# A transformer block on one core: the feed-forward weight splits in slots 10 to 15, the second statistics merge behind the residual, squares between exponentials, two low parts moved

## Chip, core and metric

The kernel runs on one core of a Trainium2 chip. The metric is the device time of one execution in microseconds; the median of three executions stands for the kernel. One more execution was recorded by the profiler, and all rows below are from it.

## What is computed

The reference takes x (128 sequences of 64 tokens, 256 features) and a condition vector for each sequence. It applies a conditioned layer norm and then one transformer block whose two halves are each modulated by the condition:

```python
x = _L0_cond_ref(x, cond_256, ...)              # layer norm, affine, + tanh(cond @ lin_w.T + lin_b)
a_alpha = (t @ attn_alpha_w.T)[:, None, :]
x = x + a_alpha * _attention(_ada_rmsnorm(x, t, attn_gamma_w, attn_beta_w), W_q, W_k, W_v, W_o)   # 16 heads of 16
f_alpha = (t @ ffn_alpha_w.T)[:, None, :]
return x + f_alpha * _swiglu(_ada_rmsnorm(x, t, ffn_gamma_w, ffn_beta_w), gate_w, hidden_w, out_w, out_b)
# _swiglu: silu(x @ gate_w.T) * (x @ hidden_w.T) @ out_w.T + out_b, 1024 hidden features
```

## The kernel before

The 8192 tokens are worked on in 32 parts of 256 tokens, four sequences each. The program of every engine is one loop over slots `s`; a slot handles one sequence of attention (two at a time, in even slots) and one of the 128 feed-forward steps, `f = s - FFN_AT` with `FFN_AT = 12`. `grp, j = s // 4, s % 4` say which part is in which stage. The order on an engine is the order of the code, and semaphores tie the engines together. The attention of part m starts in slot 4m, its feed-forward part in slot 4m + 12. So slots -8 to 11 are a lead-in with attention alone, and from slot 12 on TensorE has both. In slots below 12 (`wide(s)`) the row minimum is subtracted on VectorE (`centre`, L797) and one exponential a sequence runs on ScalarE (L1127); later eight exponentials a sequence run straight from PSUM (L1134).

All large products are made in three passes: each operand is split into a rounded high part (made on ScalarE, a copy to fp32r) and a low part, the difference (made on VectorE or GpSimd). The attention input's low part `xn_lo` is `split_lo_a` (L1344, GpSimd), the feed-forward input's is `xf_lo` (L869, VectorE).

The feed-forward weights are split in the same way, in 12 chunks of 128 x 512: 0 to 3 gate, 4 to 7 hidden, 8 to 11 output. The table `SPLITS` says in which slot: ScalarE makes the high part of a chunk at the end of its body of slot s (L1184), and VectorE the low part at the end of its body of the slot after, s + 1 (L940):

```python
for c in SPLITS.get(s if s < 0 else s - 1, ()) if s != 0 else ():
    split_ffn_weights(c)
```

TensorE waits for the low parts by the semaphore `ffn_lo_made`, which counts chunks in the table's order. `gate(0)` wants the count at chunk 6, `gate(2)` at chunk 3, and the down product of step f, for the first four steps, its own chunk:

```python
def down(f):
    m, q = f // PSEQ, f % PSEQ
    pe.wait_ge(prod_lo_made, f + 1)
    if f < PSEQ:
        pe.wait_ge(ffn_lo_made, split_no(8 + f))
```

In slot s, TensorE runs `gate(f)`, `hidden(f)` and then `down(f - 1)`. VectorE runs `activate(f)` (L876, after ScalarE's tanh L1157) and `product(f)` (L884, after hidden(f)), then token work on the input (`shift_tokens` L750 and L754, `token_stats` L716), and then the weight splits. `product_lo(f)` (L912) opens the next slot.

`merge_stats` (L723 to L733) makes mean and variance from the statistics of 512 tokens; seven instructions on 128 x 4 elements. The stage of part m in attention runs: `turn_x` on TensorE, `make_residual` (L782, VectorE), squares (L1053), their sum (GpSimd L1320) turned on TensorE (L418), their mean (L842, L845), the inverse root (GpSimd L1306), scale, beta, high part, low part. `square_f`, `sum_squares_f`, `scale_f`, L1357 and `split_hi_f` are the same for the feed-forward half; its squares are turned by L422.

Of the kernel before, what the change touches and what calls it, by code (L numbers as in the profile page):

```python
# [61 lines left out]
LAST_SLOT = FFN_AT + FFN_STEPS + 2  # L62
LAST_STEP = FFN_STEPS - 1
LATE_TURNS = (BATCH - PSEQ - 1, BATCH - 1)
SPLITS = {-3: (0, 2), -2: (4,), 1: (5,), 3: (7,), 5: (6,), 6: (8,), 9: (1,), 11: (3,), 12: (9,), 13: (10,), 14: (11,)}
SPLIT_ORDER = [c for chunks in SPLITS.values() for c in chunks]
OUT_W_AT = -3
QUAD = 32
# [3 lines left out]
def conditioned_block(nc, x, cond_t, mod_w, feat_vecs, attn_w, gate_w, hidden_w, out_w, identity, head_mask, out_t):  # L72
    with ExitStack() as ctx:
# [120 lines left out]
        def is_part(m):  # L194
            return 0 <= m < NPART

        def is_seq(g):
            return 0 <= g < BATCH
# [4 lines left out]
        def wide(g):  # L203
            return g < FFN_AT
# [505 lines left out]
        def _(dve):  # L710
# [112 lines left out]
            def attended_lo(m):  # L823
                dve.wait_ge(att_hi_made, m + 1)
                dve.tensor_tensor(kt_by_seq(att_lo[:]), attended_t, kt_by_seq(att_hi[:].bitcast(F32)), ALU.subtract
                                  ).then_inc(att_lo_made, 1)
# [35 lines left out]
            def scale_f(m):  # L862
                dve.wait_ge(inv_spread, m + 5)
                dve.wait_ge(gamma_f, m + 1)
                scale_by_rms(normed_f, PART).then_inc(scaled_f, 1)
# [97 lines left out]
            for s in range(FIRST_SLOT, LAST_SLOT):  # L963
# [23 lines left out]
                if j == 0 and is_part(grp + 2) and not PSEQ <= s <= FFN_AT and not row_part(grp + 2):  # L987
                    make_residual(grp + 2)
                if s == FFN_AT:
                    merge_stats((grp + 3) // 2, (grp + 3) // 2 + 2)  # L990
                if j == 2 and s >= 0 and is_part(grp + 2):
                    scale_a(grp + 2)
                if j == 2 and is_part(grp - 2) and not wide(s):
                    scale_f(grp - 2)
                if j == 2 and is_part(grp - 2) and wide(s):
                    scale_f(grp - 2)
                if j == 2 and is_part(grp - 1) and wide(s):
                    attended_lo(grp - 1)
                for g in (s, s + 1):
                    if s % 2 == 0 and is_seq(g) and wide(g):  # L1000
                        invert_sums(g)
# [33 lines left out]
                    shift_tokens(tile_at(s))  # L1035
                if grp % 2 == 0 and 2 <= (grp + 4) // 2 < NBLK:
                    token_stats((grp + 4) // 2, j)
                    if j == 3 and grp != 2:
                        merge_stats((grp + 4) // 2, (grp + 4) // 2 + 2)
                for c in SPLITS.get(s if s < 0 else s - 1, ()) if s != 0 else ():  # L1040
                    split_ffn_weights(c)

# [5 lines left out]
        def _(act):  # L1048
# [158 lines left out]
            for s in range(FIRST_SLOT, LAST_SLOT):  # L1207
# [27 lines left out]
                    keys_out(grp + 1)  # L1235
                if s == FFN_AT:
                    square_a(grp + 2)
                    keys_out(grp + 1)
                    square_f(grp - 2)
                if s % 2 == 0 and is_seq(s):  # L1240
                    exponentials(s)
                    if s == 2:
                        queries_out(1)
                    if wide(s) and j == 2 and is_part(grp - 1):
                        attended_hi(grp - 1)
                    if wide(s + 1):
                        exponentials(s + 1)
                if j == 0 and s >= 0 and is_part(grp + 2) and not PSEQ <= s <= FFN_AT and not row_part(grp + 2):
                    square_a(grp + 2)
                if j == 0 and is_part(grp - 2) and wide(s):  # L1250
                    square_f(grp - 2)
                if j == 2 and is_part(grp - 1) and not wide(s):
                    attended_hi(grp - 1)
                if j == 2 and PSEQ <= s < FFN_AT:
# [37 lines left out]
        def _(pool):  # L1292
# [49 lines left out]
            def split_lo_a(m):  # L1342
                pool.wait_ge(hi_a, m + 1)
                pool.tensor_tensor(xn_lo[:], normed_a[:], xn_hi[:].bitcast(F32), ALU.subtract).then_inc(lo_a, 1)  # L1344
# [42 lines left out]
            for s in range(FIRST_SLOT, LAST_SLOT):  # L1387
# [9 lines left out]
                    apply_beta_a(grp + 2)  # L1397
                for g in (s, s + 1):
                    if s % 2 == 0 and is_seq(g) and wide(g):
                        normalise_probs(g)  # L1400
                        if g == s and j == 2:
                            split_lo_a(grp + 2)
                if s == FIRST_SLOT or s == FIRST_SLOT + PSEQ:
                    sum_squares_a(grp + 2)
# [81 lines left out]
```

## Time and profile before

| | |
|---|---|
| median of three executions | 958.8 us (957.88 to 959.99) |
| profiled execution, its own time | 958.45 us |
| its span in the trace | 956.4 us |
| busy: TensorE, VectorE, ScalarE, GpSimd | 920.8, 742.4, 636.4, 499.9 us |
| TensorE busy in the first 100 us | 70.3 us |

The span is what the trace covers, from the first instruction to the last; the profiled execution's time is 2.05 us longer than its span. Times of rows are microseconds from the start of the span, durations of groups nanoseconds.

### The profile page before, as it was taken

The page shows a single profiled execution, that of the slowest core. Times are in us where ns is not written, and L with a number is a line of the kernel's source. Part 1 is how long each engine was busy: PE and PEld are TensorE (multiplying, and loading weights), DVE is VectorE, ACT ScalarE, POOL GpSimd, SP SyncE. Part 2 cuts the span into 40 slices and gives each one's busy share as a digit, 9 for nine tenths or more (in the row PEclk, how much of TensorE's full clock was granted, in tenths as well). Part 3 has the DMA queues.
Part 4 walks back from the last instruction along what each step waited for, and adds up shares of the span by engine and source line. Part 5 has one row for each costly group of instructions (what it writes and reads, how often), then busy time and mean ns, then how long its engine had stood idle before and what let it go on. Part 6 is the DMA issues. An engine that isn't in the chain of part 4 may idle for free.

```text
span 956.4 us, 28592 instructions
## 1 busy us (share of the span) xinstructions
PE 920.8 (96%) x11064; PEld 885.5 (93%) x11064; DVE 742.4 (78%) x1438; ACT 636.4 (67%) x1839; POOL 499.9 (52%) x477
## 2 busy tenths in 40 slices
PE   5668999999999999999999999999999999999998
PEld 5557999999999999999999999999999999998998
DVE  6987787788778778878877887877877787667665
ACT  3656767767776776776676677677668667666432
POOL 3596455555554555555456556555565545543320
PEclk9999999999999999999999999999999999999999
DMA  6200012110021201112121111102101011100000
GB/s 231 69 2 29 13 24 57 24 51 12 20 58 23 57 24 45 15 23 57 24 53 27 23 37 24 57 24 51 31 6 52 24 35 18 19 13 13 13 12 23
DMA packets 40630, 33.75 MB, mean 35 GB/s; under 512 B 10800, under 2 KB 39984, under 8 KB 40496
## 3 DMA queue, kind: packets, MB, share of 16 engines
q1 hardware_dynamic: 40496, 31.93, 13.6%
q8 instruction: 88, 1.44, 0.8%
q14 instruction: 46, 0.38, 0.3%
HBM read 23.37 MB, written 8.55 MB: 33 GB/s over the span
## 4 chain that ended last, share of the span: by engine, by line
PE 90%; DVE 4%; POOL 2%; issue 2%; ACT 1%; DMA 0%; SPq 0%; DVEq 0%; ACTq 0%; POOLq 0%
PE psum L375 18%; PE psum L377 18%; PE psum L376 18%; PE psum L626 6%; PE psum L625 6%; PE psum L624 6%; PE psum L539 5%; PE psum L511 4%; PE psum L555 4%; PE psum L410 2%; PE psum L429 1%; DVE least L790 1%; PE psum L422 1%; POOL probs L1371 0%; DVE row_sum L806 0%
## 5 line engine op out<-in xcount | busy, mean ns | idle before, releaser
L375 PE MATMUL psum<-xf_hi,ffn_hi 128*128 128x256 f32 x1024 | 291.2, 284 | 0.8 <-ACT probsT L1142 0.6
L376 PE MATMUL psum<-xf_lo,ffn_hi 128*128 128x256 f32 x1024 | 288.1, 281 | 0.0
L377 PE MATMUL psum<-xf_hi,ffn_lo 128*128 128x256 f32 x1024 | 287.8, 281 | 0.0
L1134 ACT ACTIVATE probs<-psum,least 128x64 f32<-128x64 f32 x928 | 205.2, 356 | 38.5 <-DVE least L790 37.7
L1371 POOL TENSOR_TENSOR probs<-probs,inv_sum 128x512 f32<-128x512 f32 x128 | 134.6, 1053 | 153.3 <-DVE inv_sum L811 153.3
L375 PEld LDWEIGHTS psum<-xf_hi,ffn_hi 128*128 128x128 f32 x1024 | 192.7, 188 | 1.7 <-issue 1.2
L376 PEld LDWEIGHTS psum<-xf_lo,ffn_hi 128*128 128x128 f32 x1024 | 192.8, 188 | 0.0
L377 PEld LDWEIGHTS psum<-xf_hi,ffn_lo 128*128 128x128 f32 x1024 | 192.7, 188 | 0.0
L1177 ACT ACTIVATE prod_hi<-late 128x512 fp32r<-128x512 f32 x127 | 83.1, 654 | 125.8 <-DVE late L884 125.5
L626 PE MATMUL psum<-prod_hi,ffn_lo 128*128 128x256 f32 x512 | 144.1, 281 | 0.0
L625 PE MATMUL psum<-prod_lo,ffn_hi 128*128 128x256 f32 x512 | 144.1, 281 | 0.0
L624 PE MATMUL psum<-prod_hi,ffn_hi 128*128 128x256 f32 x512 | 144.1, 281 | 0.0
L806 DVE TENSOR_REDUCE row_sum<-probs 128x8 f32<-128x512 f32 x128 | 87.0, 680 | 71.9 <-ACT probs L1134 71.8
L876 DVE SCALAR_TENSOR_TENSOR late<-tanh,psum 128x512 f32<-128x512 f32 x127 | 86.5, 681 | 61.0 <-ACT tanh L1157 59.9
L912 DVE TENSOR_TENSOR prod_lo<-late,prod_hi 128x512 fp32r<-128x512 f32 x127 | 92.7, 730 | 21.0 <-ACT prod_hi L1177 21.0
L1157 ACT ACTIVATE tanh<-psum 128x512 f32<-128x512 f32 x127 | 77.8, 613 | 45.7 <-PE psum L377 41.0
L1142 ACT ACTIVATE probsT<-psum 128x512 f32<-128x512 f32 x128 | 69.4, 594 | 56.0 <-PE psum L555 56.0
L1357 POOL TENSOR_TENSOR normed_f<-normed_f,mod 128x512 f32<-128x512 f32 x32 | 33.4, 1044 | 121.9 <-DVE normed_f L848 121.9
L625 PEld LDWEIGHTS psum<-prod_lo,ffn_hi 128*128 128x128 f32 x512 | 96.4, 188 | 0.0
L626 PEld LDWEIGHTS psum<-prod_hi,ffn_lo 128*128 128x128 f32 x512 | 96.4, 188 | 0.0
L624 PEld LDWEIGHTS psum<-prod_hi,ffn_hi 128*128 128x128 f32 x512 | 96.4, 188 | 0.0
L790 DVE TENSOR_REDUCE least<-psum 128x8 f32<-128x512 f32 x128 | 82.6, 683 | 16.5 <-PE psum L511 16.4
(123 smaller groups left out, 2162.0 us busy)
## 6 DMA issues: line engine op xcount, KB each, us to landing
out_t_dram<-x_res SPq DMA_DIRECT2D x31, 256.0 KB, 3.2
xin<-x_dram SPq DMA_DIRECT2D x15, 512.0 KB, 6.7
shift_tok<-shift_rows SPq DMA_DIRECT2D x104, 64.0 KB, 3.3
inv_row<-inv_rows SPq DMA_DIRECT2D x26, 128.0 KB, 4.8
w_raw<-attn_w_dram SPq DMA_DIRECT2D x1, 1024.0 KB, 8.2
x_res<-gate_w_dram SPq DMA_DIRECT2D x1, 1024.0 KB, 10.9
late<-hidden_w_dram SPq DMA_DIRECT2D x1, 1024.0 KB, 12.5
w_raw<-out_w_dram SPq DMA_DIRECT2D x1, 1024.0 KB, 6.4
```

The costliest lines, as they stand in the source:

```text
L375: pe.matmul(out, stat_hi, mov_hi, start=first, stop=False)
L376: pe.matmul(out, stat_hi, mov_lo, start=False, stop=False)
L377: return pe.matmul(out, stat_lo, mov_hi, start=False, stop=last)
L624: pe.matmul(out, ffn_hi[:, 2, cols], hi, start=first, stop=False)
L625: pe.matmul(out, ffn_hi[:, 2, cols], half(prod_lo[f % 2], u), start=False, stop=False)
L626: return pe.matmul(out, ffn_lo[:, 2, cols], hi, start=False, stop=q == 3 and u == 1 and (mt == KT - 1 or m == NPART - 1))
L790: dve.tensor_reduce(least[g % 2][:].rearrange("p (r a) -> p r a", r=4), scores[g % 2], AX_X, ALU.min).then_inc(least_made, 1)
L806: dve.tensor_reduce(row_sum[g % 2][:], probs[g % 4][:].rearrange("p (h k) -> p h k", k=SEQ), AX_X, ALU.add).then_inc(sum_made, 1)
L876: dve.scalar_tensor_tensor(out=act_gate, in0=tanh[:], scalar=1.0, in1=gate_bank, op0=ALU.add, op1=ALU.mult).then_inc(act_made, 1)
L912: dve.tensor_tensor(prod_lo[f % 2][:], prod, prod_hi[f % 2][:].bitcast(F32), ALU.subtract).then_inc(prod_lo_made, 1)
L1134: op = act.activation(probs[g % 4][:, h * SEQ:(h + 1) * SEQ], scores[g % 2][:, h // 2, h % 2], ACT.Exp, bias=least[g % 2][:, h:h + 1], sca ...
L1371: pool.tensor_tensor(by_head, by_head, inv_sum[g % 2][:].unsqueeze(2).broadcast_to([P, 8, SEQ]), ALU.mult).then_inc(probs_made, 1)
```

## The change

Five things change; nothing is added to or taken from the computation, and TensorE's instructions stand in the same order as before.

```diff
-SPLITS = {-3: (0, 2), -2: (4,), 1: (5,), 3: (7,), 5: (6,), 6: (8,), 9: (1,), 11: (3,), 12: (9,), 13: (10,), 14: (11,)}
+SPLITS = {-3: (0, 2), -2: (4,), 10: (6, 5, 7), 11: (8, 1), 12: (3,), 13: (9,), 14: (10,), 15: (11,)}
...
@@ VectorE
                 if s == FFN_AT:
-                    merge_stats((grp + 3) // 2, (grp + 3) // 2 + 2)
+                    merge_stats(3, 5)
...
+                if j == 2 and is_part(grp - 1) and wide(s):
+                    attended_lo(grp - 1)
                 if j == 2 and is_part(grp - 2) and wide(s):
                     scale_f(grp - 2)
-                if j == 2 and is_part(grp - 1) and wide(s):
-                    attended_lo(grp - 1)
...
                     token_stats((grp + 4) // 2, j)
-                    if j == 3 and grp != 2:
+                    if j == 3 and grp > 2:
                         merge_stats((grp + 4) // 2, (grp + 4) // 2 + 2)
+                if s == PSEQ:
+                    merge_stats(2, 4)
...
@@ ScalarE
                 if s == FFN_AT:
                     square_a(grp + 2)
+                    square_f(grp - 2)
                     keys_out(grp + 1)
-                    square_f(grp - 2)
...
                         attended_hi(grp - 1)
+                    if wide(s) and j == 0 and is_part(grp - 2):
+                        square_f(grp - 2)
                     if wide(s + 1):
                         exponentials(s + 1)
...
-                if j == 0 and is_part(grp - 2) and wide(s):
-                    square_f(grp - 2)
...
@@ GpSimd
                 for g in (s, s + 1):
                     if s % 2 == 0 and is_seq(g) and wide(g):
+                        if s == 2 and g == s:
+                            split_lo_a(grp + 2)
                         normalise_probs(g)
-                        if g == s and j == 2:
+                        if s == 6 and g == s or s == 10 and g == s + 1:
                             split_lo_a(grp + 2)
```

So the chunks 5, 7, 6, 8, 1, whose low parts VectorE made in slots 2, 4, 6, 7 and 10, are now made in slots 11 (6, 5, 7) and 12 (8, 1); chunk 3 goes from slot 12 to 13, and chunks 9, 10 and 11 from slots 13, 14, 15 to 14, 15, 16. The merge of the third block of tokens goes from the end of slot 3 to the end of slot 4.

The first place is VectorE around slot 16. Before, from the end of slot 15 to the end of slot 16 (`ffn_lo` is a low weight part, here chunk 11):

```order
L754 SCALAR_TENSOR_TENSOR xin<-xin,rstd,shift_tok 128x256
L940 SCALAR_TENSOR_TENSOR ffn_lo<-w_raw,ffn_hi 128x512
L912 TENSOR_TENSOR prod_lo<-late,prod_hi 128x512
L763 TENSOR_SCALAR token_inv<-token_ms 128x2
L790 TENSOR_REDUCE least<-psum 128x8 x2
L806 TENSOR_REDUCE row_sum<-probs 128x8
L811 RECIPROCAL inv_sum<-row_sum 128x8
L876 SCALAR_TENSOR_TENSOR late<-tanh,psum 128x512
L884 TENSOR_TENSOR late<-psum,late 128x512
L716 BN_STATS stats<-xin 128x6
L916 SCALAR_TENSOR_TENSOR late<-psum,vecs,mod 128x256 x2
```

The same place in the changed kernel:

```order
L940 SCALAR_TENSOR_TENSOR ffn_lo<-w_raw,ffn_hi 128x512
L912 TENSOR_TENSOR prod_lo<-late,prod_hi 128x512
L763 TENSOR_SCALAR token_inv<-token_ms 128x2
L790 TENSOR_REDUCE least<-psum 128x8 x2
L806 TENSOR_REDUCE row_sum<-probs 128x8
L811 RECIPROCAL inv_sum<-row_sum 128x8
L876 SCALAR_TENSOR_TENSOR late<-tanh,psum 128x512
L884 TENSOR_TENSOR late<-psum,late 128x512
L716 BN_STATS stats<-xin 128x6
L940 SCALAR_TENSOR_TENSOR ffn_lo<-w_raw,ffn_hi 128x512
L916 SCALAR_TENSOR_TENSOR late<-psum,vecs,mod 128x256 x2
```

The upper L940 is now chunk 10, and chunk 11 stands below slot 16's product (L884). In slots 14 and 15 chunks 9 and 10 stand in the same way, below the L884 and L754 of their slot.

The second place is VectorE in slots 11 and 12. Before, from the gated attention output (L834) to the first row minima of slot 12:

```order
L834 TENSOR_TENSOR gated_a<-psum,mod 128x512
L869 TENSOR_TENSOR xf_lo<-normed_f,xf_hi 128x512
L716 BN_STATS stats<-xin 128x6
L782 SCALAR_TENSOR_TENSOR x_res<-psum,w_sq,mod 128x256 x2
L790 TENSOR_REDUCE least<-psum 128x8 x2
```

In the changed kernel:

```order
L834 TENSOR_TENSOR gated_a<-psum,mod 128x512
L869 TENSOR_TENSOR xf_lo<-normed_f,xf_hi 128x512
L716 BN_STATS stats<-xin 128x6
L940 SCALAR_TENSOR_TENSOR ffn_lo<-late,ffn_hi 128x512 x3
L782 SCALAR_TENSOR_TENSOR x_res<-psum,w_sq,mod 128x256 x2
L790 TENSOR_REDUCE least<-psum 128x8 x2
```

Three splits stand between the low part of the feed-forward input and the residual of the next part.

The third place is GpSimd in slot 10, from beta (L1339) on. Before:

```order
L1339 TENSOR_TENSOR normed_a<-normed_a,mod 128x512
L1371 TENSOR_TENSOR probs<-probs,inv_sum 128x512
L1344 TENSOR_TENSOR xn_lo<-normed_a,xn_hi 128x512
L1371 TENSOR_TENSOR probs<-probs,inv_sum 128x512
L1357 TENSOR_TENSOR normed_f<-normed_f,mod 128x512
```

In the changed kernel, whose lines here are two further down:

```order
L1341 TENSOR_TENSOR normed_a<-normed_a,mod 128x512
L1373 TENSOR_TENSOR probs<-probs,inv_sum 128x512 x2
L1346 TENSOR_TENSOR xn_lo<-normed_a,xn_hi 128x512
L1359 TENSOR_TENSOR normed_f<-normed_f,mod 128x512
L1378 TENSOR_TENSOR x_res<-x_res,gated_a 128x2x256
```

The low part went behind the second multiplication of probabilities; in slot 2 it went ahead of the first.

## Rows read from the trace of the kernel before

**Rows 1.** The page: TensorE's busy tenths in 40 slices of the span.

```profile
PE   5668999999999999999999999999999999999998
```

**Rows 2.** Busy time by stretch: stretch, length, busy (instructions) by engine, granted clock, DMA.

```profile
0.00:100.00 100.00, 70.31 (x861) 61.76 (x862) 78.73 (x182) 57.90 (x124) 59.90 (x63) 0.97 0.24 81
100.00:200.00 100.00, 99.63 (x1212) 96.00 (x1211) 80.60 (x157) 71.21 (x214) 54.52 (x52) 1.00 0.13 27
```

**Rows 3.** Timeline (start, duration, line, operation, idle before): TensorE, keys of slot 4.

```profile
43.35 0.39 PE L375 MATMUL psum<-xn_hi,w_hi 128*128 128x256 f32 x1 [1.10 <-POOL xn_lo L1344]
```

**Rows 4.** Timeline of TensorE: three gaps in the lead-in.

```profile
30.91 0.39 PE L375 MATMUL psum<-xn_hi,w_hi 128*128 128x256 f32 x1 [2.47 <-POOL xn_lo L1344]
...
79.42 1.12 PE L539 MATMUL psum<-ident,probs 128*128 128x128 f32 x4 [2.02 <-POOL probs L1371]
...
90.59 0.41 PE L418 MATMUL psum<-ident,square_sum_a 128*128 128x128 f32 x2 [1.53 <-issue]
```

**Rows 5.** Timeline of VectorE, slots 2 to 5.

```profile
41.33 0.84 DVE L940 SCALAR_TENSOR_TENSOR ffn_lo<-late,ffn_hi 128x512 fp32r<-128x512 f32 x1
...
42.54 0.78 DVE L723 TENSOR_TENSOR merge<-stats 128x4 f32<-128x4 f32 x1
...
44.79 0.87 DVE L782 SCALAR_TENSOR_TENSOR x_res<-psum,w_sq,mod 128x256 f32<-128x256 f32 x2
...
49.84 0.96 DVE L940 SCALAR_TENSOR_TENSOR ffn_lo<-late,ffn_hi 128x512 fp32r<-128x512 f32 x1
```

**Rows 6.** Timeline of ScalarE, slots 4 and 12.

```profile
46.35 1.27 ACT L1096 ACTIVATE k_heads<-psum,pair 128x512 f32<-128x512 f32 x2
...
84.83 1.27 ACT L1096 ACTIVATE k_heads<-psum,pair 128x512 f32<-128x512 f32 x2 [0.90 <-PE psum L377]
...
86.50 1.75 ACT L1134 ACTIVATE probs<-psum,least 128x64 f32<-128x64 f32 x8
```

**Rows 7.** Timeline of VectorE, slots 11 and 12.

```profile
81.06 1.08 DVE L869 TENSOR_TENSOR xf_lo<-normed_f,xf_hi 128x512 fp32r<-128x512 f32 x1 [3.22 <-ACT xf_hi L1089]
...
82.41 0.85 DVE L782 SCALAR_TENSOR_TENSOR x_res<-psum,w_sq,mod 128x256 f32<-128x256 f32 x2
...
84.51 0.25 DVE L723 TENSOR_TENSOR merge<-stats 128x4 f32<-128x4 f32 x1
...
89.80 0.69 DVE L884 TENSOR_TENSOR late<-psum,late 128x512 f32<-128x512 f32 x1
```

**Rows 8.** Timeline of GpSimd, slots 4 to 11.

```profile
49.21 2.49 POOL L1371 TENSOR_TENSOR probs<-probs,inv_sum 128x512 f32<-128x512 f32 x2 [2.08 <-DVE inv_sum L811]
51.80 0.71 POOL L1306 TENSOR_TENSOR mean_sq<-mean_sq,minus_half 128x2 f32<-128x2 f32 x1
...
78.32 1.04 POOL L1371 TENSOR_TENSOR probs<-probs,inv_sum 128x512 f32<-128x512 f32 x1
```

**Rows 9.** Timeline of VectorE: what ends its slots 14, 15 and 16.

```profile
105.54 0.68 DVE L940 SCALAR_TENSOR_TENSOR ffn_lo<-w_raw,ffn_hi 128x512 fp32r<-128x512 f32 x1
...
112.43 0.69 DVE L940 SCALAR_TENSOR_TENSOR ffn_lo<-w_raw,ffn_hi 128x512 fp32r<-128x512 f32 x1
...
119.77 0.42 DVE L716 BATCH_NORM_STATS2 stats<-xin 128x6 f32<-128x256 f32 x1
```

**Rows 10.** Timeline of TensorE: first matmul of the down product, slots 14 to 16.

```profile
102.26 0.28 PE L624 MATMUL psum<-prod_hi,ffn_hi 128*128 128x256 f32 x1
...
107.94 0.28 PE L624 MATMUL psum<-prod_hi,ffn_hi 128*128 128x256 f32 x1
...
116.31 0.28 PE L624 MATMUL psum<-prod_hi,ffn_hi 128*128 128x256 f32 x1
```

**Rows 11.** Groups of VectorE from 98 to 940 us: mean of one in ns.

```profile
L754 DVE SCALAR_TENSOR_TENSOR xin<-xin,rstd,shift_tok 128x256 f32<-128x256 f32 x51 | 24.7, 484 | 1.8
```

**Rows 12.** TensorE behind two gaps: stretch, length, busy, mean granted clock, DMA.

```profile
31.00:35.00 4.00, 4.00 (x37) 0.57 0.00 0
79.00:83.00 4.00, 3.58 (x72) 0.57 0.05 6
```

## The prediction

> **What bounds the kernel now.** I read the page's slices first: from the sixth on TensorE stands at nine tenths [rows 1]. Then the stretches: between 100 and 200 us it is busy for 99.63, in the first 100 for 70.31 [rows 2]. From slot 12 on (about 80 us) the kernel is bound by TensorE; whatever it loses there is lost, since a stretch that is 99.6% full has no room to catch up. Before that TensorE waits, and the chain runs through VectorE, GpSimd and ScalarE. The timelines show it: the keys of part 2 wait for a low part from GpSimd [rows 3], and probabilities and token work on GpSimd make the gap before 79.42 [rows 4]. So the change has two sides: in the lead-in, slots 2 to 12, it can give time; in slots 14 to 16 it puts weight splits where TensorE needs them, and what it costs there counts in full. A difference under 0.2% of the time, some 2 us, could not be told from none.
>
> **The gain in the lead-in.** I follow the chain by what starts when, before and (estimate) now.
>
> Slots 2 to 5. One split (0.84) and the merge (from 42.54 to the residual at 44.79, 2.25) leave the way of the residual, which could start 3.1 sooner [rows 5]. Less comes through. The first exponential of slot 4 stands behind the key copies at 46.35 [rows 6], and these wait for the keys, some 1.4 us of matmuls that started at 43.35 when `xn_lo` was done [rows 3]. With its new place ahead of both multiplications `xn_lo` ends some 0.6 sooner (it waits for its high part instead of for 1.04 of GpSimd). The copies then start near 44.25, 2.1 sooner, and with them exponentials and row sums. Behind the row sums stood a split of 0.96 [rows 5]; now the merge stands there. The multiplications on GpSimd start 2.1 sooner, and the merge falls beside them. What that costs is seen in two rows: its first instruction took 0.78 beside a working GpSimd [rows 5], and 0.25 with GpSimd idle [rows 7]. I take 1.9 for the whole, the price beside GpSimd (between the 2.25 of before and some 0.9 if all ran as at 84.51). So 2.1 + 0.96 - 1.9 is about 1.2; since the two multiplications, 2.49 in the row and 2 x 1.04 = 2.08 unhindered, are also less hindered, I put the inverse root of slot 5, at 51.80 [rows 8], at 50.2: 1.6 sooner.
>
> The Trainium skill (Advanced Engine Details and Errata, VectorE Performance Modes) says that VectorE's second SBUF port is shared with GpSimd, so that instructions of GpSimd and two-port ones of VectorE block each other. The rows on the merge agree. By that rule the merge gains nothing by its new place as long as GpSimd works there; without it this step would give 1 us more.
>
> Slots 5 to 10. GpSimd works without a pause from 49 to 66 us, so 1.6 goes on, and the splits of chunks 6 and 8, which fell beside its work, no longer stretch it; that adds some 0.45 each and the order of squares between the exponentials takes 0.4 of waiting away. I carry 3 us to the end of slot 9. In slot 10 the low part moves behind the second multiplication: that one, at 78.32 [rows 8], comes sooner still, near 74, and beta of the feed-forward half, which stood right behind it, comes 3.2 sooner than before, as the order of the two does not change their sum.
>
> Slots 11 and 12. `xf_lo` at 81.06 waits for its high part [rows 7] and comes 3.2 sooner, at 77.9. But behind it stand now three splits of 0.68 [rows 9], which overlap a little when back to back: 1.9 us. VectorE was idle for 3.22 before `xf_lo`; the splits do not use that idle time, they come after it. The residual goes from 82.41 to 81.0: of 3.2 only 1.4 is left. From there to the first exponential of slot 12 it was 4.1 us before (82.41 to 86.50 [rows 6, 7]), of which 0.9 was a wait of the key copies for keys that are now long there [rows 6]; so it starts at 81.0 + 3.2 = 84.2, 2.3 to 2.4 sooner. The product of step 0, 89.80 before [rows 7], and TensorE's next work, 90.59 [rows 4], come **2.4 us sooner**. Bounds: nothing, if the three splits and contention eat all; 4.5, if what GpSimd gains came through whole. The two splits of slot 12 fall behind product 0 and delay the mean (L842) by 0.7 beside a gate product of 1.4: hidden.
>
> **The cost in slots 14 to 16.** Before, chunk 9's low part was made a slot ahead of its use. Now down(1) in slot 14 needs chunk 9, which VectorE makes at the end of slot 14, behind product(2); this needs hidden(2), which stands right ahead of down(1) on TensorE. Nothing else stands between them there, and all of TensorE's later work is queued behind down(1).
>
> Slot 14: down(1) began at 102.26 [rows 10]; the split that stood at the end of that slot ended at 105.54 + 0.68 = 106.22 [rows 9]. Stall: **4.0**.
>
> Slot 15: down(2). From 102.26 to 107.94 TensorE did four products of 12 matmuls [rows 10], 1.42 each; hidden(3) ends as late as it always did behind its gate product. Behind it come product (0.69), `xf_lo` (0.7), a shift pair (2 x 0.48 [rows 11]) and the split (0.68): **3.0**. With the old contention it would be 112.43 + 0.69 - 107.94 = 5.2 [rows 9, 10].
>
> Slot 16: down(3) began at 116.31 and the statistics ended at 119.77 + 0.42; with the split 120.87, 4.5 later [rows 9, 10]. But VectorE came late into that slot: TensorE began it at 107.94 + 1.42 = 109.36, VectorE was on slot 15 until 112.43 + 0.69 = 113.12, 3.8 into it. Now it ends slot 15 when down(2) begins, before slot 16. Most of the 3.8 it will wait for the new scores; I count 1.5 of it as won. **3.0**, at most 4.5.
>
> Sum 10.0. The small waits that TensorE had between 100 and 200 us, 0.37 [rows 2], fall in slot 17 and vanish: 9.6.
>
> **The clock.** Behind gaps of 2.47 and 2.02 us [rows 4] TensorE's granted clock was 0.57 in the mean of four microseconds [rows 12]: it fell from 2.4 to 1.2 GHz for most of them, which loses 4 x 0.43 = 1.7 us of work. Behind the gap of 1.53 [rows 4] I saw no fall. The stalls of 4.0, 3.0 and 3.0 are all longer than the gaps that did it, and a gap of 2.5 before 88 is likely as well, since TensorE's own work comes 4 us sooner and product 0 only 2.4. A low stretch that begins within a gap costs less, so of four I take two full losses, **3.4**; bounds 0 and 6.8 (four).
>
> Sum: 958.45 - 2.4 + 9.6 + 3.4 = 969.05 on the profiled execution; the median lies 0.35 above that one, so **969 us**. The extremes are 958.8 - 4.5 + 9.6 = 964 with the best lead-in and no fall of the clock, and with the worst in each 958.8 + 13.3 + 6.8 = 979.
>
> **The rivals.**
> - The stalls come but the clock stays: 966. For it: the gap of 1.53 brought no fall, and each stall might come out a third shorter; against: both longer gaps in the lead-in brought the fall. 0.2.
> - The lead-in gives nothing, because the three splits and VectorE's order hold the residual of slot 12 where it was: 971.5, and with contention in slots 15 and 16 as before 975. For it: only 1.4 of 3.2 is left on paper. 0.2.
> - Faster: the lead-in gives more than the stalls take. TensorE is idle for 29.7 of the first 100 us, about half of it in slots 2 to 12. The mechanism would be that each us off GpSimd's chain comes through, and no split is waited for on VectorE. It decides once the gain passes 9.6, four times my ledger; at the 10 to 11 that the idle time could give at most it is 957. Against it: the first divergence is at 41 us and the three splits alone take back 1.9. 0.03.
> - No change, because the wait of down(f) for its chunk is met in time: VectorE would have to make the split before product(2); its order shows that it doesn't. With only the gap of the lead-in it would be 956.5, and with half of the stalls met near 960. 0.03.
>
> **How the numbers follow.** My forecast, with stalls of 9 to 11, gain of 1 to 4 and clock of 1.7 to 5, has 0.54 and spans 965 to 973. To it come the two slower rivals; I leave out the two small ones and the far end. Range 963 to 975. Slower by over 0.2%: 0.94; within: 0.03; faster: 0.03.
>
> **What would show it.** The keys of slot 4 near 42.7, the residual of slot 12 near 81, TensorE's squares near 88.2. Three gaps before the down product (L624) in slots 14, 15, 16 of 4, 3 and 3 us, each released by `ffn_lo`, with a granted clock of half behind at least two. Wrong would be: gaps under 2 us there; a start of the squares later than 90; or a TensorE that is idle in later slots, since no work there has changed.

## The result: 12 us slower, and the profile after

The changed kernel takes 970.93 us (median of four executions, 969.99 to 973.84) against 959.14 for the kernel before beside it; the ratio is 1.013, with a 95% interval of 1.0116 to 1.0144. Its profiled execution took 970.32 us, 11.9 more than that of before, with a span of 968.5 us, 12.1 more.

The page of the changed kernel: busy tenths and granted clock in slices, then the group of the down product's first pass (busy, mean ns, idle before).

```profile
PE   5777789999999999999999999999999999999998
...
PEclk9999899999999999999999999999999999999999
...
L624 PE MATMUL psum<-prod_hi,ffn_hi 128*128 128x256 f32 x512 | 144.5, 282 | 9.7 <-DVE ffn_lo L940 9.7
```

Against [rows 1] the fifth slice (97 to 121 us) went from 9 to 7 and the sixth from 9 to 8, and the granted clock of the fifth is 8 tenths: that is where the loss lies. The group says what it is: 9.7 us of idle time ahead of L624, all of it released by a low weight part.

The timeline of the changed kernel's TensorE, from the keys of slot 4 to slot 18, and a slot's first L539 near the end:

```profile
42.97 0.36 PE L375 MATMUL psum<-xn_hi,w_hi 128*128 128x256 f32 x1 [0.67 <-ACT v_diag L1117]
...
88.90 0.41 PE L418 MATMUL psum<-ident,square_sum_a 128*128 128x128 f32 x2 [2.52 <-issue]
...
95.15 1.03 PE L539 MATMUL psum<-ident,probs 128*128 128x128 f32 x8
...
106.18 0.36 PE L624 MATMUL psum<-prod_hi,ffn_hi 128*128 128x256 f32 x1 [3.94 <-DVE ffn_lo L940]
...
116.71 0.36 PE L624 MATMUL psum<-prod_hi,ffn_hi 128*128 128x256 f32 x1 [3.05 <-DVE ffn_lo L940]
118.67 1.91 PE L539 MATMUL psum<-ident,probs 128*128 128x128 f32 x8
...
129.57 0.36 PE L624 MATMUL psum<-prod_hi,ffn_hi 128*128 128x256 f32 x1 [2.71 <-DVE ffn_lo L940]
...
136.99 1.03 PE L539 MATMUL psum<-ident,probs 128*128 128x128 f32 x8
...
881.27 1.04 PE L539 MATMUL psum<-ident,probs 128*128 128x128 f32 x8
```

The same regions of before, first L539 of slots 14, 16 and 18 and of the slot near the end:

```profile
95.33 1.03 PE L539 MATMUL psum<-ident,probs 128*128 128x128 f32 x8
...
109.37 1.03 PE L539 MATMUL psum<-ident,probs 128*128 128x128 f32 x8
...
124.47 1.21 PE L539 MATMUL psum<-ident,probs 128*128 128x128 f32 x8
...
869.11 1.04 PE L539 MATMUL psum<-ident,probs 128*128 128x128 f32 x8
```

The squares of slot 13 come 1.7 us sooner than the 90.59 of [rows 4]. The three gaps before L624 are 3.94, 3.05 and 2.71, 9.70 in all. The first L539 of an even slot marks how far TensorE is. So the changed kernel is 0.2 ahead at slot 14, 9.3 behind at 16, 12.5 behind at 18, and 12.2 behind at the end: the whole difference arises within 30 us, and in the 740 us after it less than half a microsecond is caught up.

TensorE in five stretches of the changed kernel (length, busy and instructions, granted clock, DMA):

```profile
88.00:92.00 4.00, 3.10 (x20) 0.79 0.00 0
92.00:96.00 4.00, 4.00 (x29) 0.78 0.00 0
108.00:110.00 2.00, 2.00 (x11) 0.50 0.01 3
118.00:120.00 2.00, 2.00 (x12) 0.50 0.10 9
130.00:132.00 2.00, 2.00 (x19) 1.00 0.04 8
```

The granted clock is at 1.2 GHz in part of slot 13 and again behind the first and the second stall, and stays at 2.4 GHz behind the third. From the squares of slot 13 to slot 14 it is 6.25 us (88.90 to 95.15) against 4.74 before (90.59 to 95.33): the clock takes back 1.5 of the 1.7 that were won. Between slot 14 and slot 18 TensorE loses 12.7 us (0.18 + 12.52), of which 9.7 are gaps; 3.0 are left for two low stretches, less the 0.4 of small waits that no longer arise.

VectorE in the changed kernel: slots 11 and 12, then the product of slot 14 and the split of slot 16.

```profile
78.26 1.11 DVE L869 TENSOR_TENSOR xf_lo<-normed_f,xf_hi 128x512 fp32r<-128x512 f32 x1 [3.34 <-ACT xf_hi L1091]
...
79.63 1.87 DVE L940 SCALAR_TENSOR_TENSOR ffn_lo<-late,ffn_hi 128x512 fp32r<-128x512 f32 x3
81.43 0.86 DVE L782 SCALAR_TENSOR_TENSOR x_res<-psum,w_sq,mod 128x256 f32<-128x256 f32 x2
...
84.52 0.97 DVE L727 TENSOR_SCALAR mean<-merge 128x4 f32<-128x4 f32 x1
85.47 1.02 DVE L730 TENSOR_SCALAR merge<-merge 128x4 f32<-128x4 f32 x1
...
103.83 0.69 DVE L884 TENSOR_TENSOR late<-psum,late 128x512 f32<-128x512 f32 x1
128.75 0.67 DVE L940 SCALAR_TENSOR_TENSOR ffn_lo<-w_raw,ffn_hi 128x512 fp32r<-128x512 f32 x1
```

GpSimd and ScalarE in the changed kernel, the rows that answer to 51.80 in [rows 8] and to 86.50 in [rows 6]:

```profile
50.73 0.71 POOL L1308 TENSOR_TENSOR mean_sq<-mean_sq,minus_half 128x2 f32<-128x2 f32 x1 [1.19 <-DVE mean_sq L845]
```

```profile
84.52 1.75 ACT L1136 ACTIVATE probs<-psum,least 128x64 f32<-128x64 f32 x8
```

The lead-in is shorter, and part of it goes again: the three splits take 1.87 us ahead of the residual, and in slot 12 the merge, now beside a working GpSimd, holds VectorE from 83.4 to 86.6, where the row sums of slot 12 begin.

### The profile page after: what moved, and what is told of

It reads as the page before. It is cut to its first block, busy times and chain, and to the rows that moved or that the text cites. A ratio compares the mean times of both kernels' runs of the same rounds, so it can differ in the third digit from the quotient of the medians.

```text
span 968.5 us, 28592 instructions
## 1 busy us (share of the span) xinstructions
PE 926.1 (96%) x11064; PEld 890.7 (92%) x11064; DVE 741.9 (77%) x1438; ACT 635.9 (66%) x1839; POOL 497.7 (51%) x477
## 4 chain that ended last, share of the span: by engine, by line
PE 90%; DVE 3%; ACT 2%; POOL 2%; issue 2%; DMA 0%; SPq 0%; ACTq 0%; DVEq 0%; POOLq 0%
PE psum L375 18%; PE psum L377 18%; PE psum L376 18%; PE psum L624 6%; PE psum L626 6%; PE psum L625 6%; PE psum L539 5%; PE psum L511 4%; PE psum L555 4%; PE psum L410 2%; PE psum L429 1%; PE psum L422 1%; DVE ffn_lo L940 1%; POOL probs L1373 1%; ACT probs L1136 0%
## 5 line engine op out<-in xcount | busy, mean ns | idle before, releaser
L624 PE MATMUL psum<-prod_hi,ffn_hi 128*128 128x256 f32 x512 | 144.5, 282 | 9.7 <-DVE ffn_lo L940 9.7
L624 PEld LDWEIGHTS psum<-prod_hi,ffn_hi 128*128 128x128 f32 x512 | 96.6, 189 | 10.2 <-issue 10.2
## 6 DMA issues: line engine op xcount, KB each, us to landing
x_res<-gate_w_dram SPq DMA_DIRECT2D x1, 1024.0 KB, 10.6
```

The costliest lines, as they stand in the source:

```text
L624: pe.matmul(out, ffn_hi[:, 2, cols], hi, start=first, stop=False)
```

## The experiments

Each kernel ran beside the kernel before on the same chip, in three to five rounds; a ratio is to that kernel, with its 95% interval. "Before" is the kernel ahead of the change, "after" the changed one. A lead-in is compared by the time from slot 1's first mean (L842) to slot 13's squares (L418), since what comes ahead of that mean varies by up to 2.3 us from execution to execution. Here is that mean in VectorE's timeline of before, and then of after:

```profile
34.66 0.42 DVE L842 TENSOR_REDUCE square_mean<-psum 128x2 f32<-128x256 f32 x1 [1.59 <-PE psum L418]
```

```profile
34.73 0.42 DVE L842 TENSOR_REDUCE square_mean<-psum 128x2 f32<-128x256 f32 x1 [1.28 <-PE psum L418]
```

So the lead-in is 90.59 - 34.66 = 55.93 us before and 88.90 - 34.73 = 54.17 after, 1.8 shorter. Traces of kernels that are alike up to there agree in it to 0.03 us (54.14 to 54.17 in four of them).

### The late splits taken back

After, with chunks 9, 10 and 11 a slot earlier, as before; everything else of the change stays.

```diff
-SPLITS = {-3: (0, 2), -2: (4,), 10: (6, 5, 7), 11: (8, 1), 12: (3,), 13: (9,), 14: (10,), 15: (11,)}
+SPLITS = {-3: (0, 2), -2: (4,), 10: (6, 5, 7), 11: (8, 1), 12: (3, 9), 13: (10,), 14: (11,)}
```

> The changed kernel with only chunks 9, 10 and 11 back in slots 12, 13 and 14 (low parts in 13, 14, 15). Theory of the late chunks: the three gaps before the down product go (3.9, 3.1 and 2.7 us in the changed kernel), and with them the falls of the clock behind them; what stays is the gain of 1.7 us at the squares of slot 13 less the fall of the clock in that slot, so TensorE enters slot 14 where the kernel before does, within half a microsecond, and the time is 957.5 to 959. Rival, that the bunched splits of slots 11 to 13 or the moved instructions cost time of their own: 961 or more.

959.31 us, ratio 0.9996 (0.9986 to 1.0005). The stalls are gone and with them the whole loss, 11.6 us. But the kernel isn't faster than before, which I had expected it to be. Its TensorE, and a stretch behind the squares:

```profile
89.00 0.41 PE L418 MATMUL psum<-ident,square_sum_a 128*128 128x128 f32 x2 [2.54 <-issue]
...
95.25 1.04 PE L539 MATMUL psum<-ident,probs 128*128 128x128 f32 x8
```

```profile
90.00:91.00 1.00, 1.00 (x7) 0.50 0.00 0
```

The squares come 1.6 us sooner (lead-in 54.15), and slot 14 starts 0.1 sooner: the clock fell behind the gap of 2.54 in slot 13, and the time from the squares to slot 14 is 6.25 again; at 94 us it is back at 2.4 GHz.

### The splits alone

Before, with the new SPLITS table and nothing else (the same line as in the change's diff).

> The kernel before with only the table of splits changed. Theory: the three gaps are there in full (9 to 10 us), and the lead-in gives less than in the changed kernel, because the merge is still ahead of the residual and the low part of slot 10 between the multiplications: squares of slot 13 at 89.5 to 90.6, time 970 to 972.5. Rival, that the moved instructions had a share in the loss: under 969.

972.42 us, ratio 1.0131 (1.0116 to 1.0146): the table alone brings the whole loss. The same three gaps, 3.94, 3.05 and 2.71, stand before L624. The squares stand at 89.00, with slot 1's mean at 34.19, so the lead-in is 54.81, 1.1 shorter. That number can't be compared with before and after as it stands. In this profiled execution and in that of the next kernel the clock fell near 37 us, behind slot 1's mean, while in all the others it fell between 30 and 33 us, ahead of it. The mean came early, and the instruction behind it, L845, took 0.91 us beside GpSimd in place of 0.17. The next step, the inverse root of slot 1 on GpSimd, is a fairer start; here it is before, and then with the table alone:

```profile
35.37 0.80 POOL L1306 TENSOR_TENSOR mean_sq<-mean_sq,minus_half 128x2 f32<-128x2 f32 x1 [0.74 <-DVE mean_sq L845]
```

```profile
35.64 0.80 POOL L1306 TENSOR_TENSOR mean_sq<-mean_sq,minus_half 128x2 f32<-128x2 f32 x1
```

From it to the squares it is 55.22 us before, 53.47 after (35.43 to 88.90) and 53.36 with the table alone. So by this start the table gives the whole gain of the lead-in, and by the other 1.1 of 1.8. One trace doesn't settle which. In slot 13 its clock didn't fall, but it fell behind all three stalls, the third time here (TensorE's stretches around the gap of 2.71):

```profile
120.00:130.00 10.00, 7.29 (x87) 0.95 0.13 15
130.00:140.00 10.00, 10.00 (x130) 0.88 0.07 23
```

From slot 13 on there are three falls here and three in after, in other places, and the loss is the same.

### The other moves alone

After, with the SPLITS table of before.

> The changed kernel with the old table of splits: only the merge, the squares and the two low parts are moved. Theory: no gap before the down product; the lead-in gives 1 to 3 us at the squares of slot 13, since GpSimd's chain is shorter and no three splits stand before the residual of slot 12: 956 to 958.5. Rival, that without the splits out of the way the moves give nothing: 958.5 to 959.5; rival, that a move costs on its own: over 960.

960.69 us, ratio 1.0009 (1.0000 to 1.0019): no gain, where I had expected 1 to 3 us. Squares at 90.98, slot 1's mean at 34.47, lead-in 56.51, 0.6 longer than before; but from the inverse root of slot 1 (35.92) it is 55.06, 0.2 shorter. By either number the moves alone are worth next to nothing. VectorE shows a reason:

```profile
51.93 0.68 DVE L940 SCALAR_TENSOR_TENSOR ffn_lo<-late,ffn_hi 128x512 fp32r<-128x512 f32 x1
```

With the old table a split still stands behind row sums and merge, ahead of the mean that GpSimd's chain waits for: merge and split are now both in that place (L842 follows at 52.53). That the merge's move is worth something only once the split is gone fits this, but isn't shown by one trace.

### One stall in place of three

After, with only chunk 9 late.

```diff
-SPLITS = {-3: (0, 2), -2: (4,), 10: (6, 5, 7), 11: (8, 1), 12: (3,), 13: (9,), 14: (10,), 15: (11,)}
+SPLITS = {-3: (0, 2), -2: (4,), 10: (6, 5, 7), 11: (8, 1), 12: (3,), 13: (9, 10), 14: (11,)}
```

> As the run with chunks 9 to 11 back, but chunk 9 alone stays late (slot 13, low part in slot 14). Theory: one gap of 3.9 us before the down product of slot 14, none in slots 15 and 16, and a fall of the clock behind it that costs up to 1.7: 4 to 5.6 us over that run. Rival, that the gaps of slots 15 and 16 come from the first one and not from their own chunks: gaps there too, 8 us or more over it.

963.45 us, ratio 1.0043 (1.0026 to 1.0059), 4.1 over the kernel with no late chunk. Its down product in slot 14, and two stretches:

```profile
106.23 0.55 PE L624 MATMUL psum<-prod_hi,ffn_hi 128*128 128x256 f32 x1 [3.95 <-DVE ffn_lo L940]
```

```profile
89.00:97.00 8.00, 6.58 (x96) 1.00 0.00 0
102.00:112.00 10.00, 6.05 (x30) 0.68 0.06 14
```

One gap of 3.95 and none in slots 15 and 16: each late chunk makes its own stall. From 102 to 112 us the clock is low for 6.4 us of ten (0.68 is 1 - 0.64/2), about twice as long as behind the other stalls; the first 0.6 of it still lies in the gap, so it costs some 3 us of work. And in slot 13, behind a gap of 2.53 as in the first experiment, it didn't fall (1.00 from 89 to 97). This profiled execution took 965.22 us, the longest of the four, 1.8 above their median; it is about what gap and fall were expected to give, while the medians, 4.1 apart, leave hardly more than the gap of 3.95. So the other executions either lost less to the clock here or had more of its falls in the kernel with no late chunk.

### The three splits in VectorE's idle time

The first experiment's kernel (no late chunk), with the three low parts of slot 11 ahead of `xf_lo`, where VectorE had been idle for 3.34 us.

```diff
@@ VectorE
+                if s == 11:
+                    for c in SPLITS[10]:
+                        split_ffn_weights(c)
                 if j == 3 and is_part(grp - 2) and s < BATCH:
                     ffn_split_lo(grp - 2)
```

(and `s not in (0, 11)` at the end of the body)

> The run with chunks 9 to 11 back, and VectorE makes the three low parts of slot 11 ahead of xf_lo in place of behind it, in the 3.3 us in which it waits for the high part. Theory (the three splits behind xf_lo hold the residual of slot 12): the residual comes 1.8 us sooner, near 79.7, and the squares of slot 13 1 to 1.8 sooner, near 87.5; time 957 to 958.5 against 959.3. Rival (the residual is not what the product of step 0 waits for, but ScalarE's order or the keys): residual sooner, squares within 0.4 of 89.0, time unchanged. Either way a longer gap of TensorE before the squares may bring a fall of the clock worth 1.5, which can hide the gain.

959.06 us, ratio 0.9991 (0.998 to 1.0003). The lead-in is 88.72 - 34.88 = 53.84, 0.3 shorter and not the 1 to 1.8 that I had expected. VectorE, then GpSimd in the same stretch:

```profile
75.87 4.52 DVE L940 SCALAR_TENSOR_TENSOR ffn_lo<-late,ffn_hi 128x512 fp32r<-128x512 f32 x3 [0.82 <-ACT ffn_hi L1189]
80.32 0.68 DVE L869 TENSOR_TENSOR xf_lo<-normed_f,xf_hi 128x512 fp32r<-128x512 f32 x1
81.26 0.85 DVE L782 SCALAR_TENSOR_TENSOR x_res<-psum,w_sq,mod 128x256 f32<-128x256 f32 x2
```

```profile
76.66 1.49 POOL L1362 TENSOR_TENSOR normed_f<-normed_f,mod 128x512 f32<-128x512 f32 x1
78.11 1.74 POOL L1381 TENSOR_TENSOR x_res<-x_res,gated_a 128x512 f32<-128x512 f32 x1
```

Three splits that take 1.87 us with GpSimd idle take 4.52 beside it, and stretch GpSimd's instructions in turn: the same two take 1.04 and 1.29 in after. Counted from slot 1's mean, `xf_lo` is 1.9 us later than in after, and the residual 0.3 sooner. The idle time was no free room: it lay beside GpSimd's work. The Trainium skill (GPSIMD Engine Reference, Key points) says that GpSimd contends with those of VectorE's instructions that run in a 2-port mode or take two SBUF inputs; a split takes two, and these rows agree.

### The low parts back

The first experiment's kernel, with `split_lo_a` between the two multiplications again in slots 2 and 10 (in slot 6 the change had left it there).

```diff
@@ GpSimd
-                        if s == 2 and g == s:
-                            split_lo_a(grp + 2)
                         normalise_probs(g)
-                        if s == 6 and g == s or s == 10 and g == s + 1:
+                        if g == s and j == 2:
                             split_lo_a(grp + 2)
```

> The run with chunks 9 to 11 back, with the two low parts back between the multiplications of slots 2 and 10. Prediction's ledger: the new places gave 0.6 in slot 2 and 1.7 in slot 10 on the way to xf_lo of which the splits took most; so squares up to 0.5 to 1 later. Rival: the splits' leaving gives all of the lead-in, the low parts nothing: squares within 0.3 of 89.0 and the time within 0.1%.

958.36 us, ratio 0.9988 (0.9975 to 1.0002). The lead-in is 54.17 against 54.15: moving the low parts is worth nothing at the squares. The clock fell at 52 us in the one trace and at 77 us in the other, so those falls don't show at the squares either.

### The merge back

The first experiment's kernel, with the merge of the third block at the end of slot 3 again.

```diff
@@ VectorE
-                    if j == 3 and grp > 2:
+                    if j == 3 and grp != 2:
                         merge_stats((grp + 4) // 2, (grp + 4) // 2 + 2)
-                if s == PSEQ:
-                    merge_stats(2, 4)
```

(The change turned this round; here it is turned back.)

> The run with chunks 9 to 11 back, with the merge of the third block back at the end of slot 3, ahead of the residual. Prediction's ledger: the merge's new place is worth about half a microsecond, since it meets GpSimd at either place; with it back the inverse root of slot 5 comes 0.3 to 0.8 later and the squares likewise. Rival: no difference in the squares, time within 0.1%.

959.8 us, ratio 1.0003 (0.9992 to 1.0014). The lead-in is 91.53 - 36.47 = 55.06, 0.9 longer. VectorE there:

```profile
52.27 1.02 DVE L845 TENSOR_SCALAR mean_sq<-square_mean 128x2 f32<-128x2 f32 x1
```

Counted from slot 1's mean, L842 (at 51.85) comes at the same time as in the first experiment (15.38 against 15.30), but the L845 behind it now takes 1.02 beside GpSimd's multiplication, where it took 0.17 in after. So in these two traces the merge's place is worth 0.9 us, once the splits are gone, and by another way than I had worked out. With the table alone, where the merge is at the old place as well, L845 took 1.02 too.

### Slot 12's merge behind the product

The kernel with the splits ahead, and the merge of slot 12 moved behind product 0.

```diff
@@ VectorE
-                if s == FFN_AT:
-                    merge_stats(3, 5)
...
                     activate(f)
                     product(f)
+                if s == FFN_AT:
+                    merge_stats(3, 5)
```

> The previous run with the merge of slot 12 moved from before the row sums to behind product 0. In the changed kernel that merge took from 83.4 to 86.7 beside GpSimd's multiplications, and the row sums began at 86.6. Theory: activation and product of step 0 come 0.4 to 0.7 sooner than in the previous run, time 0.3 to 0.7 less. Rival: ScalarE's exponentials and tanh set it, nothing changes.

958.48 us, ratio 0.9988 (0.9978 to 0.9998). Lead-in 53.56, another 0.3 shorter, a little under the 0.4 to 0.7 expected: the merge beside GpSimd at 83 to 87 us had cost that much. But it doesn't reach slot 14. Behind the product the merge holds up the next mean (L842), and TensorE waits 0.56 for it at 90.98; slot 14 starts at 93.91, 59.10 behind slot 1's mean, where in the kernel with the splits ahead it was 93.50 and 58.62.

### The late splits, as early as they can be

After with its three late chunks, but each low part right behind the product of its slot, ahead of the token work.

```diff
@@ VectorE
                     activate(f)
                     product(f)
+                if s in (14, 15, 16):
+                    for c in SPLITS[s - 1]:
+                        split_ffn_weights(c)
```

(and `s not in (0, 14, 15, 16)` at the end of the body)

> The changed kernel with the low parts of chunks 9, 10 and 11 made right behind the product of slots 14, 15 and 16, ahead of the token work and xf_lo. Theory (the stall is product, then whatever stands between product and split on VectorE, then split): the gap of slot 14 shrinks by the shift pair from 3.9 to 3.0, that of slot 15 by pair and xf_lo from 3.05 to 1.5, that of slot 16 by the statistics from 2.7 to 2.35; sum 6.9 in place of 9.7. And behind the gap of 1.5 the clock does not fall, which gives up to 1.5 more: 2.8 to 4.5 us under the changed kernel, 966.5 to 968. Rival (the gaps are set by something else, ScalarE or a counted wait): gaps as they were.

968.17 us against 960.84 for before in the same call, ratio 1.0069 (1.0052 to 1.0086). TensorE, then the stretch around each gap:

```profile
105.30 0.36 PE L624 MATMUL psum<-prod_hi,ffn_hi 128*128 128x256 f32 x1 [3.03 <-DVE ffn_lo L940]
...
114.28 0.36 PE L624 MATMUL psum<-prod_hi,ffn_hi 128*128 128x256 f32 x1 [1.53 <-DVE ffn_lo L940]
...
125.25 0.36 PE L624 MATMUL psum<-prod_hi,ffn_hi 128*128 128x256 f32 x1 [2.37 <-DVE ffn_lo L940]
```

```profile
102.00:112.00 10.00, 6.97 (x47) 0.83 0.04 14
112.00:122.00 10.00, 8.47 (x125) 1.00 0.02 2
122.00:132.00 10.00, 7.63 (x52) 0.83 0.16 15
```

The gaps are the ones worked out from VectorE's order, to 0.03 us: what stands between the product and the split on VectorE is the length of the stall. The clock fell behind 3.03 and behind 2.37, not behind 1.53; with gaps of 6.93 TensorE is 9.9 later at slot 18 than at slot 14, which leaves 3.0 for two falls, or 1.7 each by the stretches (0.83 in the mean of ten microseconds), less some small waits that vanish. In slot 18 (134.20) this trace is 2.8 ahead of after, the difference of the gaps; the clock gave nothing back, since it fell twice here too. It fell in slot 13 as well, behind a gap of 2.53.

### A smaller gap in slot 13

The first experiment's kernel, with gate(1) ahead of the turned squares on TensorE in slot 13, which splits the gap.

```diff
@@ TensorE
+                if f == 1:
+                    gate(f)
                 if j == 1 and is_group(grp) and s >= 0:
                     norm_bank_free(s)
                     turn_squares(grp)
                 if is_step(f) and f < LAST_STEP:
-                    gate(f)
+                    if f != 1:
+                        gate(f)
                     hidden(f)
```

> The run with chunks 9 to 11 back, and on TensorE the gate product of step 1 stands ahead of the turned squares of slot 13. It takes nothing out; it shortens the gap of 2.5 us before the squares to 1.8. Theory of the clock (the fall in slot 13 took back 1.5 of the 1.8 us that the lead-in gave): no fall behind the shorter gap, slot 14 starts 1.5 sooner in the trace, median 0.7 to 1.5 less than 959.3, since not every execution need have had the fall. Rival: the fall does not hang on that gap, or the gain is lost elsewhere: 959.3 as before.

959.1 us (957.19 to 962.48), ratio 1.0 (0.9987 to 1.0012). Its TensorE:

```profile
88.34 0.39 PE L375 MATMUL psum<-xf_hi,ffn_hi 128*128 128x256 f32 x1 [1.76 <-DVE late L879]
...
94.30 1.04 PE L539 MATMUL psum<-ident,probs 128*128 128x128 f32 x8
```

The gap is 1.76, and a second one of 0.88 follows at 91.34, where TensorE waits for the mean of the squares. The clock didn't fall, and slot 14 starts 1.0 sooner than before. Yet the median isn't below that of before, so the rival's number came. Nor is it shown that the shorter gap kept the clock up: in five of ten traces it stayed up behind the whole gap of 2.2 to 2.55 as well, and against such a trace (the low parts back, slot 14 at 93.73, 58.95 behind slot 1's mean) this kernel starts slot 14 later, 59.34 behind it.

### A version from the results

After with no late chunk; `5` and `1` a slot later, so that only two splits stand ahead of slot 12's residual; slot 12's merge behind the product; and gate(1) ahead of the squares.

```diff
+SPLITS = {-3: (0, 2), -2: (4,), 10: (6, 7), 11: (8, 5), 12: (1, 3, 9), 13: (10,), 14: (11,)}
```

> A version that should beat both: the moved merge, squares and low parts; chunks 9 to 11 in time; only two splits (6, 7) behind xf_lo, chunk 5 in slot 12; the merge of slot 12 behind product 0; and the gate product of step 1 ahead of the turned squares of slot 13, so that TensorE waits for the activation (0.7 us earlier) and not for the product. Theory: residual 0.6 sooner, product 0.6 to 0.9 sooner, and no fall of the clock in slot 13: 956 to 957.5 against 959.4. Rival: the gains in the lead-in lengthen a gap elsewhere and a fall of the clock takes them back: 958 to 959.5.

958.67 us against 959.35, ratio 0.999 (0.9982 to 0.9999), and not the 956 to 957.5 expected: it is what the rival said. Its TensorE:

```profile
87.25 0.39 PE L375 MATMUL psum<-xf_hi,ffn_hi 128*128 128x256 f32 x1 [1.47 <-DVE late L879]
...
93.56 1.03 PE L539 MATMUL psum<-ident,probs 128*128 128x128 f32 x8
```

As in the kernel before this one, a second gap follows, 1.27 at 90.64, for the mean of the squares. Slot 14 starts 1.8 us sooner than before; near the end (869.31 against 869.11) nothing of it is left. It beats both kernels, the changed one by 12 us and the one before by 0.1%, which is at the edge of what can be told.

## Why the prediction came out right

**The stalls** were forecast as 4.0, 3.0 and 3.0 and measured 3.94, 3.05 and 2.71: 9.7 against 10.0. The step rests on one reading: TensorE's order has only hidden(f) between the product's input and the down product, so everything on VectorE between product and split is a stall. The kernel with the table alone shows that the table makes them, the first experiment that without the late chunks the loss is gone, and the one with split and product neighbours that the stall has exactly the length of what stands between. In slot 16 the split ended at 128.75 + 0.67 = 129.42; I took 1.5 of VectorE's lateness as won, 1.8 was.

**The clock** was sized as two full losses of 1.7, 3.4. The trace has three falls: 1.5 in slot 13, and 3.0 in slots 14 to 16 once the 0.4 of small waits is set against them, so 3.4 without, 4.9 in all. The term is right in kind, 1.5 too small. How many falls an execution has, and what one costs, isn't fixed: 1.5 to 1.7 in most, some 3 in the kernel with one stall.

**The lead-in** was the weakest term: 2.4 forecast, 1.7 measured at the squares (1.8 from slot 1's mean). The way points came as forecast: the inverse root of slot 5 at 50.73 (50.2), `xf_lo` at 78.26 (77.9), the residual of slot 12 at 81.43 (81.0), the exponentials at 84.52 (84.2), each 0.3 to 0.5 late. The rest, from 2.0 at the exponentials to 1.7 at the squares, I put down to slot 12's merge: I had left it out of the sum, and beside GpSimd it took 3.2 us and put off the row sums; moved away, it gave 0.3. Two parts of the working were wrong though their sum was near, which is luck. I gave the low part's new place in slot 2 the first 0.6 us, and slot 10 another 0.2; both together are worth 0.0. I took the keys to come forward to 42.7, and they came to 42.97, for they then waited for ScalarE (L1117) and not for the low part. And I counted the merge's move as a gain that contention takes away; with the splits gone it is worth 0.9, since it keeps L845 away from GpSimd's multiplication. How the 1.8 divides between table and moves stays open: the table alone gives 1.1 or 1.9, the moves alone lose 0.6 or give 0.2, by the start from which one counts. No run takes back the order of the squares, or that of `scale_f` and `attended_lo`, by itself.

**The sum.** Forecast: -2.4 + 9.6 + 3.4 = 10.6. By the trace: -1.7 at the squares, +1.5 clock in slot 13, +9.7 stalls, +3.0 clock less small waits, 12.5 at slot 18; 12.1 by the spans, 11.9 by the times. At slot 18 that is 1.9 over the forecast: 0.7 from the lead-in, 1.5 from the clock, -0.3 from the stalls; the measured median is 1.9 above 969.05 too.

**The rivals.** "The clock stays" fell: it was low three times. "The lead-in gives nothing", at 971.5, lies nearer to the measured 970.93 than my 969, but not by its mechanism: the residual of slot 12 came 1.0 sooner and the squares 1.7, and then a fall of the clock in slot 13 took 1.5 of it, behind a gap that before was 1.53 long and is now 2.52 because TensorE's own work comes sooner than the product. "Faster" and "no change" fell with the stalls.

**What stays open.** In kernels without late chunks, apart from the one with the moves alone, the lead-in gains 0.9 to 2.4 us (by the time to the squares), slot 14 starts up to 1.8 sooner, and the medians stand 0.1 to 1.2 below those of before, or at most 0.2 above. From slot 18 to the end single traces drift by up to 1.4 us against one another (the first experiment: 0.05 ahead at slot 18, 1.3 behind at the end; the one with gate(1) ahead: 0.9 ahead and 0.8 ahead). Which part of that belongs to a kernel, and which to an execution, one trace of each can't tell. The clock isn't the cause of that drift: none of the 13 traces has a low stretch behind 140 us. But part of the spread goes with it. Of 81 executions of before that ran beside these kernels, the 36 with a mean granted clock of 0.991 to 0.994 have a median of 960.2 us, the 45 at 0.995 or 0.996 one of 959.1. In the same round, at 0.996 alone, before had a median of 959.35 (9 executions), gate(1) ahead 958.84 (9) and the last kernel 958.49 (7): with the clock alike, the two stand 0.5 and 0.9 below before.

## What to carry to other kernels

When a split, copy or other preparation is moved later, look at the engine that needs it: if it is full from there on, the stall is the whole run of instructions between the last shared event and the preparation, and it is never caught up; its length can be read from two rows before anything is run. An idle stretch of VectorE beside GpSimd's work isn't room for instructions that read two operands; there both engines lose what the move was to win. And a gain ahead of an engine's own queue may only lengthen that engine's gap: ask what the longer gap can do to its clock before counting the gain, and compare traces only where the clock fell in the same places.

## What the hardware showed that I hadn't expected

- VectorE and GpSimd stretch one another by more than I had taken: three splits of 128x512 took 4.52 us in place of 1.87, GpSimd's additions of 128x512 beside them 1.49 and 1.74 in place of 1.04 and 1.29. Even instructions on 128x4 and 128x2 elements, 0.15 to 0.17 us elsewhere, took 0.69 to 1.02; among them L727, L730 and L845, which have one tensor operand each. Two SBUF inputs alone would not say why these three are long; the 2-port mode that the Trainium skill (GPSIMD Engine Reference, Key points) names beside them might, but no run here tells in which mode they ran.
- Behind gaps of 2.2 to 2.55 us in slot 13 TensorE's clock fell in five profiled executions (after, the late splits taken back, the other moves alone, the merge back, and the late splits as early as they can be) and not in five others (the splits alone, one stall, the splits in idle time, the low parts back, slot 12's merge behind the product), with nearly the same work around them. From slot 13 on there was no fall behind gaps of up to 1.76, and always one behind those of 3.03 and more; there was one behind 2.37 (the late splits as early as they can be); behind 2.71 there was none in after, and one in the kernel with the splits alone.
- In the lead-in the length of the gap decides as little. Behind the same gap of 2.48 us near 52 us the clock fell in six traces and not in three (the splits in idle time, the low parts back, slot 12's merge behind the product), though the kernels differ by at most one low part's place up to there. And it fell behind gaps of no more than 1.57, 1.57 and 1.58 in three traces (at 77 us with the splits alone and with the low parts back, at 69 us with the late splits as early as they can be), where other traces with the same gap show no fall.
